# Pair-wide row maxima with four score banks, merged value runs, and work moved ahead in three places

## The reference

```python
q, k, v = proj(Wq, bq), proj(Wk, bk), proj(Wv, bv)          # of layernorm(x), heads split
idx = clip(pos[None, :] - pos[:, None], -20, 20) + 20
attn1 = einsum('bhqd,bhkd->bhqk', q, k)
attn2 = einsum('bhqd,qkd->bhqk', q, rel_k[idx])
attn = softmax((attn1 + attn2) / scale, axis=-1)
w1 = einsum('bhqk,bhkd->bhqd', attn, v)
w2 = einsum('bhqk,qkd->bhqd', attn, rel_v[idx])
x = x + (w1 + w2) @ Wo.T + bo
x = x + (silu(xn @ wg.T) * (xn @ wu.T)) @ wd.T              # xn = layernorm(x), weights int8 / 127
```

## Time and profile before

| | us |
|---|---|
| median of 3 runs (1424.68 to 1428.78) | 1425.4 |
| the profiled execution, its time | 1427.91 |
| its span | 1426.0 |
| PE busy (share of the span) | 1281.4 (90%) |
| DVE busy | 948.1 (66%) |
| ACT busy | 758.8 (53%) |
| POOL busy | 550.8 (39%) |

### The profile page before, as it was taken

One profiled execution on the slowest core, in us unless ns is written; L12 is line 12 of the kernel. 1 busy time (PEld: TensorE's weight loads), 2 busy tenths in 40 slices (PEclk: granted clock), 3 DMA queues, 4 the chain that ended last, 5 costly groups with the idle time before them and its releaser, 6 DMA issues. The chain is left out here.

```text
span 1426.0 us, 67609 instructions
## 1 busy us (share of the span) xinstructions
PE 1281.4 (90%) x30680; PEld 941.6 (66%) x30688; DVE 948.1 (66%) x1844; ACT 758.8 (53%) x1413; POOL 550.8 (39%) x983
## 2 busy tenths in 40 slices
PE   4377669999999999999999999999999999889998
PEld 2244337777777777777777776777777777656665
DVE  6499777776766766766767667667767676055554
ACT  4276526565655655655656556556556566422222
POOL 4376533543435343435334353434344343022221
PEclk9689859999999999999999999999999999989999
DMA  4445420202020202112020202021120200122321
GB/s 138 114 168 183 155 57 8 53 23 63 9 64 20 53 20 55 25 48 53 20 63 13 64 20 53 21 54 30 43 55 21 64 9 9 41 60 67 89 67 45
DMA packets 101541, 79.08 MB, mean 55 GB/s; under 512 B 13256, under 2 KB 97032, under 8 KB 101256
## 3 DMA queue, kind: packets, MB, share of 16 engines
q1 hardware_dynamic: 101256, 74.77, 19.1%
HBM read 45.90 MB, written 27.26 MB: 51 GB/s over the span
## 5 line engine op out<-in xcount | busy, mean ns | idle before, releaser
L1039 DVE TENSOR_REDUCE b_mx<-b_a 128x1 f32<-128x512 f32 x1024 | 658.7, 685 | 239.2 <-PE b_a L806 233.8
L1000 ACT ACTIVATE b_p<-b_s 128x512 f32<-128x512 f32 x1024 | 569.8, 595 | 417.5 <-PE b_s L847 332.8
L897 PE MATMUL b_pv<-b_p,vg 128*16 128x128 f32 x8192 | 286.8, 275 | 0.0
L770 POOL TENSOR_TENSOR qd<-q,one 48x512 bf16<-48x512 bf16 x256 | 266.1, 1040 | 30.1 <-POOLq L286 5.3
L747 POOL TENSOR_TENSOR b_np<-vg,one 128x16 bf16<-128x16 f32 x192 | 39.1, 264 | 581.1 <-DVE b_mx L1039 570.3
L847 PE MATMUL b_s<-qd,z 112*128 112x32 bf16 (+1 forms) x6016 | 248.9, 189 | 2.8 <-issue 2.8
L806 PE MATMUL b_a<-k,q 48*128 48x512 bf16 x1024 | 203.6, 394 | 28.2 <-DVE b_mx L1039 12.6
L847 PEld LDWEIGHTS b_s<-qd,z 112*128 112x128 bf16 x6016 | 206.0, 99 | 15.2 <-issue 5.3
L897 PEld LDWEIGHTS b_pv<-b_p,vg 128*16 128x16 f32 x8192 | 196.3, 96 | 21.1 <-issue 0.2
L832 PE MATMUL b_s<-q,k 54*128 54x64 bf16 (+3 forms) x4608 | 187.8, 201 | 6.8 <-issue 3.3
L832 PEld LDWEIGHTS b_s<-q,k 54*128 54x128 bf16 (+1 forms) x4608 | 126.2, 95 | 92.2 <-PE b_s L832 29.2
(11 more groups left out here) (125 smaller groups left out, 1312.7 us busy)
## 6 DMA issues: line engine op xcount, KB each, us to landing
x<-in_x SPq DMA_DIRECT2D x32, 256.0 KB, 3.1
scratch_qop<-a_parts SPq DMA_DIRECT2D x16, 384.0 KB, 2.5
scratch_kop<-a_parts SPq DMA_DIRECT2D x16, 384.0 KB, 3.1
k<-scratch_kop SPq DMA_DIRECT2D x32, 192.0 KB
q<-scratch_qop SPq DMA_DIRECT2D x32, 192.0 KB
scratch_v<-a_vr SPq DMA_DIRECT2D x16, 256.0 KB, 3.2
k<-scratch_kop SPq DMA_DIRECT2D x32, 128.0 KB
q<-scratch_qop SPq DMA_DIRECT2D x32, 128.0 KB
```

The source lines that it names most:

```text
L770: nc.gpsimd.tensor_tensor(dst, src, one, ALU.mult).then_inc(s["qd_ready"], 1)
L897: nc.tensor.matmul(PV[32 * a:32 * a + V16, g * P:(g + 1) * P], v[:, 0 if t <= i else 1, t, h, :], PR[at.c % 2][:, t, h, :], start=(t == 0 ...
L1000: nc.scalar.activation(out, src, ACT.Exp, scale=SCALE).then_inc(s["p_ready"], 1)
L1039: nc.vector.tensor_reduce(MX[v.c % 2][:, h:h + 1], PA[(n + hp) % NBANK][:, :], AX_X, ALU.max, negate=True).then_inc(s["a_used"], 1)
```

## The change

- Attend, banks: 4 score banks in one tensor `b_s`; row pairs get one two-bank tensor `b_a`. DVE takes the maxima of both heads of a pair in one instruction over 2x512 elements. A pair may start only when the pair before it has been reduced; the odd ones of the first 8 pairs use two score banks instead.
- Attend, places: the pairs of a unit stand at the places of a table SPOTS, by i: START (where they were in a chunk) or END (behind the chunk's scores).
- Attend, values: tile 3 of the unit before moves from c = 0 to c = 1, directly ahead of the relative values; tiles 0 and 1 run as one run of 64 at c = 5.
- Attend, loads: one operand load behind each of 12 chunks (c = 0 to 5 of i = 0 and of i = 1), each behind a wait for the chunk's first scores; the value loads behind c = 6 of i = 0.
- Project: statistics, deviation and x load one batch further ahead (three instead of two); ACT normalises batch n + 2 ahead of the projections of n + 1. The x load of batch 2 stands behind the tenth of the late constant loads.
- Output: the attention transposes and their copy move ahead of the down products and of the row transposes' copy.

```diff
-NBANK = 3
+NBANK = 4
@@ stage_project, SP
-            for dst, src in late:
+            for n, (dst, src) in enumerate(late):
                 sp.dma_start(dst, src).then_inc(s["late"], 16)
+                if n == 9:
+                    sp.wait_ge(s["xn"], 1)
+                    load_x(at0(2))
...
-                if at.plus(2).exists():
-                    sp.wait_ge(s["xn"], at.count(1, 1))
-                    load_x(at.plus(2))
+                if at.plus(3).exists():
+                    sp.wait_ge(s["xn"], at.count(1, 2))
+                    load_x(at.plus(3))
@@ stage_project, ACT
+                if at.plus(2).exists():
+                    normalised(at.plus(2))
                 if at.plus(1).exists():
                     projected(at.plus(1))
-                if at.plus(2).exists():
-                    normalised(at.plus(2))
@@ stage_project, POOL; DVE likewise with statistics
-                if at.plus(2).exists():
-                    deviation(at.plus(2))
+                if at.plus(3).exists():
+                    deviation(at.plus(3))
@@ stage_attend
-    SC = [m.ps(f"b_s{n}", [P, S]) for n in range(NBANK)]
-    PA = [m.ps(f"b_a{n}", [P, S]) for n in range(NBANK)]
+    SR = m.ps("b_s", [P, NBANK, S])
+    SC = [SR[:, n, :] for n in range(NBANK)]
+    PA = m.ps("b_a", [P, HP, S])
...
+    START, END = 0, 1
+    SPOTS = (((0, START), (1, START), (1, END), (2, START), (3, START), (4, START), (5, END), (6, START)),
+             ((0, START), (1, END), (2, START), (2, END), (3, START), (4, START), (5, END), (6, START)),
+             ((0, START), (2, START), (3, START), (4, START), (5, START), (5, END), (6, START), (7, END)),
+             ((0, START), (2, START), (3, START), (4, START), (5, END), (6, START), (7, START), (7, END)))
...
+    def pair_banks(n):
+        return SR[:, 0:HP, :] if n < HH and n % 2 else PA[:, :, :]
+    def pairs_done(n):
+        return n - 1 if n <= HH else n
@@ stage_attend, SP
+                def chunk(c):
+                    sp.wait_ge(s["s_ready"], at.count(NSR, 2 * c + 1))
                 if ahead and i == 0:
-                    sp.wait_ge(s["s_ready"], at.count(NSR))
-                    operands(first, range(0, 3))
+                    for c in range(3):
+                        chunk(c)
+                        operands(first, range(c, c + 1))
                 if ahead and i == 1:
-                    operands(first, range(9, 12))
+                    for c in range(3):
+                        chunk(c)
+                        operands(first, range(c + 6, c + 7))
                 if at.plus(1).exists():
                     guard_rows(at.plus(1))
...
@@ stage_attend, PE
-                if n + HP > NBANK:
-                    pe.wait_ge(s["a_used"], n + HP - NBANK)
+                if pairs_done(n) > 0:
+                    pe.wait_ge(s["a_used"], pairs_done(n))
...
-                        if c == 0:
+                        if c == 1:
                             value_products(before, T - 1)
...
-                    if c == 4:
+                    if c == 5:
                         value_products(at, 0)
-                    if c in (5, 6):
-                        value_products(at, 1, range(H // NQ4)[2 * (c - 5):2 * (c - 4)])
+                        value_products(at, 1)
@@ stage_attend, DVE
-                for hp in range(HP):
-                    h = 2 * hh + hp
-                    dve.wait_ge(s["a_ready"], n + hp + 1)
...
-                    nc.vector.tensor_reduce(MX[v.c % 2][:, h:h + 1], PA[(n + hp) % NBANK][:, :], AX_X, ALU.max,
-                                            negate=True).then_inc(s["a_used"], 1)
+                dve.wait_ge(s["a_ready"], HP * (n + 1))
...
+                nc.vector.tensor_reduce(MX[v.c % 2][:, 2 * hh:2 * hh + HP], pair_banks(n), AX_X, ALU.max,
+                                        negate=True).then_inc(s["a_used"], 1)
@@ stage_output, PE (ACT likewise with transposed_attention ahead of transposed_rows)
                     gate_and_up(at, c)
+                if at.plus(2).exists():
+                    attention_transposes(at.plus(2))
                 for c in range(FC):
                     down(at, c)
                 if after.exists():
                     row_transposes(after)
-                if at.plus(2).exists():
-                    attention_transposes(at.plus(2))
```

More of the change, by code:

```diff
@@ L466, in deviation @@
                 nc.gpsimd.tensor_tensor(tmp["shift"][:, :], tmp["less"][:, :], tmp["rstd"][:, :], ALU.mult).then_inc(s["shift"], 1)
-            deviation(at0(0))
-            deviation(at0(1))
+            for b in range(3):
+                deviation(at0(b))
             def step(at):
@@ L561, in _ @@
             ins.then_inc(s["blank"], 1)
-            for b in range(2):
+            for b in range(3):
                 statistics(at0(b))
@@ L582, in step @@
                 maxima(1)
-                if at.plus(2).exists():
-                    statistics(at.plus(2))
+                if at.plus(3).exists():
+                    statistics(at.plus(3))
                 maxima(2)
@@ L633, in stage_attend, with pairs_beside @@
     EARLY = HH // 2
-    order = [(0, hh) for hh in range(HH)] + [(1, hh) for hh in range(EARLY)]
[L635 to L639, removed]
+    START, END = 0, 1
[3 more added lines that the diff above has]
+             ((0, START), (2, START), (3, START), (4, START), (5, END), (6, START), (7, START), (7, END)))
+    def pairs_beside(u, c, side):
+        left = [(1, EARLY + c)] * (u == 0 and side == START and c < HH - EARLY)
+        return left + [(u + LEAD, hh) for hh, spot in enumerate(SPOTS[u % T]) if spot == (c, side) and u + LEAD < U]
+    order = [(0, hh) for hh in range(HH)] + [(1, hh) for hh in range(EARLY)]
+    for u in range(U):
+        for c in range(SUB):
+            order += pairs_beside(u, c, START) + pairs_beside(u, c, END)
     place = {pair: n for n, pair in enumerate(order)}
-    def pairs_beside(at, c):
-        u = at.count()
-        return [(1, EARLY + c)] * (u == 0 and c < HH - EARLY) + [(u + LEAD, c)] * (u + LEAD < U)
+    def pair_banks(n):
+        return SR[:, 0:HP, :] if n < HH and n % 2 else PA[:, :, :]
+    def pairs_done(n):
+        return n - 1 if n <= HH else n
     def window(t, i):
@@ L705, in unit @@
                 if ahead and i == 0:
-                    operands(first, range(3, 6))
+                    for c in range(3, 6):
+                        chunk(c)
+                        operands(first, range(c, c + 1))
+                    chunk(6)
                     sp.wait_ge(s["w_ready"], at.count(1))
                     load_values(sp, k, d, at.it * 2 + at.c // T + 1, (at.c // T + 1) % 2)
-                    operands(first, range(6, 9))
+                if ahead and i == 1:
+                    for c in range(3, 6):
+                        chunk(c)
+                        operands(first, range(c + 6, c + 7))
                 if at.count() == 4 * T:
@@ L735, in link @@
                     pool.wait_ge(s["guard"], at.count(NGD, n))
-                pool.wait_ge(s["a_used"], HP * (place[at.count(), HH - 1] + 1))
+                pool.wait_ge(s["a_used"], place[at.count(), HH - 1] + 1)
                 if i == 0:
@@ L884, in scores @@
                 relative_scores(at, c).then_inc(s["s_ready"], 2)
+                row_pairs_ahead(at, c, END)
             def value_products(at, t, groups=range(H // NQ4)):
@@ L1032, in row_max @@
             def row_max(v, hh):
-                n = HP * place[v.count(), hh]
-                for hp in range(HP):
-                    h = 2 * hh + hp
-                    dve.wait_ge(s["a_ready"], n + hp + 1)
-                    if h == 0 and v.since(2):
-                        dve.wait_ge(s["guard"], v.count(NGD, 1 - 2 * NGD))
-                    nc.vector.tensor_reduce(MX[v.c % 2][:, h:h + 1], PA[(n + hp) % NBANK][:, :], AX_X, ALU.max,
-                                            negate=True).then_inc(s["a_used"], 1)
+                n = place[v.count(), hh]
+                dve.wait_ge(s["a_ready"], HP * (n + 1))
+                if hh == 0 and v.since(2):
+                    dve.wait_ge(s["guard"], v.count(NGD, 1 - 2 * NGD))
+                nc.vector.tensor_reduce(MX[v.c % 2][:, 2 * hh:2 * hh + HP], pair_banks(n), AX_X, ALU.max,
+                                        negate=True).then_inc(s["a_used"], 1)
             def keep_values(at):
@@ L1066, in unit @@
                 for c in range(SUB):
-                    for u, hh in pairs_beside(at, c):
-                        row_max(at.plus(u - at.count()), hh)
+                    for side in (START, END):
+                        for u, hh in pairs_beside(at.count(), c, side):
+                            row_max(at.plus(u - at.count()), hh)
                     if before.exists():
```

24 lines of the change are left out of this document (12 added, 12 removed).

## The result

The changed kernel takes 1497.8 us (median of 4 runs, 1494.86 to 1500.44) against 1426.1 for the kernel before beside it: a ratio of 1.050, 95% interval 1.0473 to 1.0526. It is 72 us slower; the prediction was 1412, faster, in a range of 1382 to 1436.

The account below looks back on a forecast made before the run. PE's order of work in the attend stage was taken to set the end. Loads -23, steady state +23, attend start +3, project -4 and output -12.3 sum to -13.3; 1425.4 - 13.3 = 1412 us, range 1382 to 1436.

Parts of the forecast that it names:

- Loads one to a chunk: Attend: spreading 12 loads over some 28 us stops backlogs adding up; takes 23 of 26.1 us, bounds 0 and -26.1.
- the pair loop: Attend, slower rival: the wait for each pair's reduction; PE's longer stops might lower the clock, +24 us; chance 0.10.
- The "issue" wait: Attend, beside burst loads: PE lacks instructions, which come by the same DMA engines; 26.1 us of loss over 14 batches.
- One reduction a pair: Attend: reduction takes 1.21 us and the next pair waits for the whole 1.69 us loop; +3.7 us a batch.
- Merged runs: Attend: value runs merged, three fewer visits between matmul kinds a unit at 0.21 us each; -2.6 us a batch.
- moved pairs: Attend: 8 instead of 12 of a batch's 32 pairs stand free, others cost 0.23 us; +0.9 us a batch.
- fourth bank: Attend: a fourth score bank removes 1.2 us of ACT's waits a batch and 0.7 come; -0.5 us a batch.
- Steady state: Attend: per-batch terms for merged runs, moved pairs, reduction and fourth bank sum to +1.5 us, x 15.5 = +23.
- loop rules: Attend, slower rival: the pair loop at 1.36 us a reduction, +33, 1445 us; clean distances over 65.5; chance 0.10.
- Project: Project stage: ACT's normalising leaves PE's path, only last steps gain, hole before x stays; -4 us, bounds +3 and -10.
- Output: Output stage: output projection follows row transposes at once, saving 0.88 us x 14 = -12.3, bounds -12.3 and -8.

Follow-up runs that it names:

- e1: The changed kernel with the attend stage's operand and value loads back in their old places; 1446.85 us, ratio 1.0149.
- e2: The kernel before with only the change's project and output stages, attend stage as before; 1405.11 us, ratio 0.9863.
- e8: e2 with operand loads spread but finished sooner, by c = 2 of i = 1, values behind c = 4 of i = 1; 1391.84 us, ratio 0.9767.
- e10: e1 with each pair's reduction reading only 256 of 512 columns of each head; 1388.66 us, ratio 0.9749.
- e4: The changed kernel with three score banks, three row-pair banks and one reduction a head; new places and merged value runs kept; 1557.33 us, ratio 1.0944.
- e5: The kernel before with only the new places of the operand and value loads; 1470.44 us, ratio 1.0315.
- e11: The changed kernel with each q load issued as single slots of 64 KB at the same places; 1455.2 us, ratio 1.0221.

## Why the prediction was wrong

It missed by 85.8 us. By its own terms:

- *Loads one to a chunk*, forecast -23: **the step that failed** is "The last load goes out at c = 5 of i = 1, over 4 us before the first row pair that needs it; small loads land in that." The 4 us were nearly right, counted from the scores of c = 5, which are done at 435.7; but the issue itself takes 0.8 of them. From its end at 436.46 to the due time at 439.7 there are only 3.2 us, and the landing, for which the sum had no term, took 6.0. The price is 51 us (after minus e1) where -23 was forecast, 74 of the 85.8. The pieces of it: 40.4 us of waits, and most likely the clock behind them for the rest (71.7 us at 1.2 GHz for 13.7 in e1); no run separates the two. The rows before could have warned: issuing three q loads took SP 7.04 us, so their transfers were anything but quick; I read that as a backlog of the burst and took the size of a load (64 to 192 KB) for its speed. No rival had the mechanism either: "a transfer that lands too late" was priced nowhere, and a fall of the clock behind a stop only under the pair loop.
- The "issue" wait as PE lacking instructions beside the loads: the excess falls from 19.5 (e2) to 11.1 (e8) by spreading, so more than half of it stays where I had taken away 88% (23 of 26.1). The Trainium skill ("Runtime: NRT & Kernel Launch", Instruction fetch mechanics) has the crossing of a block as mostly hidden, which would leave this excess as it is; the runs disagree in part. What makes up the rest is open. That it is instructions which PE lacks can be read from the DMA packets of the kernel before. In the 6.7 us ahead of the stop of the earlier trace rows (403.1 to 409.8) no packet of the instruction queue q8 moves, where one of 16 KB comes every 4.4 us otherwise (median); from 409.8 to 412.8, at the height of the burst, there is one, from 409.84 to 411.11, and PE goes on at 412.80:

```profile
q1 hardware_dynamic: 517, 0.53, 37.7%
...
q1 hardware_dynamic: 584, 0.51, 84.0%
q8 instruction: 1, 0.02, 2.6%
```

  (The first row is of the first window, the other two of the second: share of the 16 engines' time last.) All nine "issue" stops of over 1 us in the window of the earlier trace rows look so: the last q8 packet started 4.7 to 8.6 us after the one before it, and PE goes on 1.3 to 1.8 us after its end. This is read from one trace; no run tests it.
- *One reduction a pair*: forecast 1.21 us and 3.7 a batch, +57 over the stage and +3 at its start. Measured 1.223 us, and 58 us (e1 minus e10). PE waits for it in 104 places, not in hundreds. The worst place was where I had put it, the END pair of c = 5, i = 0: timelines of PE and DVE in the changed kernel.

```profile
1269.47 0.42 PE L875 MATMUL b_s<-qd,z 112*128 112x16 bf16 x10
1269.73 0.63 PE L964 MATMUL b_mi<-ident,b_xt 128*128 128x128 f32 x4
1270.84 0.39 PE L834 MATMUL b_a<-k,q 48*128 48x512 bf16 x2 [0.47 <-DVE b_mx L1066]
1271.05 0.62 PE L860 MATMUL b_s<-q,k 54*128 54x128 bf16 x16
1271.28 1.23 DVE L1066 TENSOR_REDUCE b_mx<-b_a 128x2 f32<-128x1024 f32 x1
1272.56 0.39 PE L834 MATMUL b_a<-k,q 48*128 48x512 bf16 x2 [0.89 <-DVE b_mx L1066]
```

  From pair to pair it is 1.72 us (1270.84 to 1272.56), the sum 1.69 of the prediction and a little; it stops PE 0.47 at c = 4 (forecast 0.41) and 0.89 at c = 5 (forecast 1.06).
- *Merged runs, moved pairs, fourth bank*: forecast -2.6 + 0.9 - 0.5 = -2.2 a batch (the first term, 3 x 0.21 x 4, is 2.5 if worked out), -34 over the stage; the second, smaller error, as e10 is only 16 us below e2. With the loop short, the clean batch is 62.7 in e10 against 63.0: -0.3. The change between kinds of matmul wasn't removed but replaced. PE's timeline in the changed kernel, ten relative scores followed by a row pair or by far scores:

```profile
1241.12 0.42 PE L875 MATMUL b_s<-qd,z 112*128 112x16 bf16 x10
1241.47 0.65 PE L860 MATMUL b_s<-q,k 54*128 54x64 bf16 x16
1242.05 0.42 PE L875 MATMUL b_s<-qd,z 112*128 112x16 bf16 x10
1242.40 0.39 PE L834 MATMUL b_a<-k,q 48*128 48x512 bf16 x2
```

  The ten take 0.35 here and 0.26 ahead of L964 above (1269.47 to 1269.73). Sixteen take 0.59 ahead of a pair and 0.50 ahead of more scores of their kind. There are 15 such places a batch in the changed kernel (relative scores followed by a pair or by far or beside scores) and none in the kernel before, where another product stands at each. 15 x 0.09 = 1.3 of the missing 1.9. That is read from timelines, not tested by a run. And no run prices the fourth bank alone; e4 and its 103 us of waits show only that the new order needs it.
- *Steady state*, forecast 63.0 + 1.5 a batch: 65.6 in e1 (66.0 by its usual distances), by its own criterion "loop rules" (over 65.5), though not for the loop's sake. The forecast distances 15.2, 14.1, 16.2, 18.9 were 15.5, 13.9 (usually 14.2), 16.7, 19.6.
- *Project*, forecast -4 with the hole kept: the stage is 7.3 shorter, and the hole is 18.62 us.
- *Output*, forecast -12.3: 13.3 measured, and the gap before the projection is gone. PE's timeline of one step of the changed kernel, which answers to the earlier trace rows:

```profile
1415.82 0.60 PE L1177 MATMUL c_pa<-ident,xa 128*128 128x128 f32 x4
1416.25 2.84 PE L1210 MATMUL c_po<-wd,c_hh 128*128 128x128 f32 x24
1418.93 0.60 PE L1193 MATMUL c_pt<-ident,c_xn 128*128 128x128 f32 x4
1419.37 1.06 PE L1185 MATMUL c_py<-wo,c_aT 128*128 128x128 f32 x8
```

  c_py starts 0.44 behind c_pt, as worked out. Both stages together: e2, -20 for a forecast of -16.

The sum closes: -20 (e2), +42 (e1 minus e2) and +51 (after minus e1) are +73 for a measured 72. Against the forecast that is -4 for the two outer stages (-20 for -16), +16 for the attend stage without its loads (+42 for +26), where the loop came out as forecast and the gains beside it were too large, and +74 for the loads: 86. Open are the excess from 0 to 1 that stays with spread loads (10 to 11 us), and how much of the loads' price is the clock: in e5 the waits of 35.5 us come with a loss of 54.6.

## What to carry to other kernels

A load that is moved later has to be checked against the time from its issue to its landing, read from rows of the same load or bounded from its transfer rate, and not guessed from its size; the first user's due time minus the last issue is the number to compare. Delay can be paid twice, as a stop of a few us may let the clock fall behind it (here 11 of 14 did). And where a run of one kind of matmul is taken out between two others, the price of the change between those two comes in its place: subtract it from the saving.

## What the runs showed of the hardware

- A load whose source repeats one part n times moves on about n DMA engines: a share of 3.2 engines at 72 GB/s for n = 3 and 2.2 at 49 for n = 2, some 22 GB/s each. Cut into single slots the last one lands 2.6 us sooner (3.4 us for 6.0), which was worth 43 us here (e11).
- A stop of PE can be followed by a granted clock of 0.50, that is 1.2 GHz (0.54 and 0.50 from 442 to 444 in the changed kernel, behind 2.8 us). The length alone doesn't decide it: of the 14 stops of 2.0 to 3.6 us for the loads 11 had such a fall behind them and one of 2.62 had none; of e11's 11, up to 1.9 us, one had (the longest, 1.87 us, before 770.41); in the kernel before one of 1.65 had the earlier trace rows and one of 2.14 (before 742.85) had not.
- An instruction packet of 16 KB that comes late, amid a burst of loads at 84% of the DMA engines' time, leaves PE standing for 1.65 us (before 412.80 in the kernel before).
- A reduction over two PSUM banks in one instruction takes 1.223 us for 1024 elements a partition, 0.15 less than two of 0.685. The line through 512 and 640 elements gives 1.197, so that the second bank adds at most some 0.03.
